# Attention's sums kept with heads on partitions, the division moved into the feed-forward on GpSimd

## The reference

```python
attend = (dist <= WINDOW) | glb[:, None] | glb[None, :]      # WINDOW = 128, glb: token 0
weights = softmax(where(attend, q @ k.T * SCALE, -inf))
x = x + (weights @ v) @ Wo.T                                 # q, k, v from layernorm(x)
h = bitlinear(xn, w_fc) + gate * (xn @ v.T @ fast_b.T @ u.T) # xn = layernorm(x)
x = x + bitlinear(relu(h) ** 2, w_proj)                      # bitlinear: ternary weights, scaled
```

## Time and profile before

| | |
|---|---|
| time, median of 3 runs (lowest to highest) | 1069.56 us (1068.85 to 1069.68) |
| the profiled execution | 1071.5 us |
| its span, first to last instruction | 1068.9 us |
| projection / attention / feed-forward, by TensorE's work | to about 190 / 190 to 702 / 702 to 1069 us |
| busy over the span: TensorE, VectorE, ScalarE, GpSimd | 1031.5, 921.4, 775.2, 699.6 us |
| mean granted TensorE clock | 0.995 of full speed |

### The profile page before, as it was taken

One profiled execution on the slowest core, in us unless ns is written; L12 is line 12 of the kernel. 1 busy time (PEld: TensorE's weight loads), 2 busy tenths in 40 slices (PEclk: granted clock), 3 DMA queues, 4 the chain that ended last, 5 costly groups with the idle time before them and its releaser, 6 DMA issues.

```text
span 1068.9 us, 40083 instructions
## 1 busy us (share of the span) xinstructions
PE 1031.5 (97%) x16071; PEld 789.2 (74%) x16071; DVE 921.4 (86%) x3202; ACT 775.2 (73%) x1328; POOL 699.6 (65%) x945
## 2 busy tenths in 40 slices
PE   9999999799999999999999999999999999999997
PEld 8888887466665666557665666588888888888886
DVE  7889987799999999999999999487888888888885
ACT  7989987687888888887888878854566554556554
POOL 3575556688888888898888888843344443344443
PEclk9999999899999999999999999999999999999999
DMA  6999989878667766776677653512122221123001
GB/s 210 263 314 276 286 231 267 155 136 154 129 139 156 157 126 137 158 145 130 139 138 160 131 120 70 143 38 80 59 89 90 60 60 60 60 79 95 26 21 40
DMA packets 187019, 142.33 MB, mean 133 GB/s; under 512 B 61625, under 2 KB 186577, under 8 KB 186833
## 3 DMA queue, kind: packets, MB, share of 16 engines
q1 hardware_dynamic: 186832, 139.77, 55.3%
HBM read 87.98 MB, written 50.95 MB: 130 GB/s over the span
## 4 chain that ended last, share of the span: by engine, by line
PE 60%; DVE 11%; issue 4%; SPq 3%; ACT 2%; DMA 1%; POOL 0%; DVEq 0%; ACTq 0%
PE e_psum L1616 13%; PE e_psum L1638 12%; PE e_psum L1347 9%; PE e_psum L1906 6%; PE e_psum L1908 6%; DVE a_masked L1362 4%; PE e_psum L1888 3%; PE e_psum L1887 3%; DVE n_stats L144 2%; DVE f_x L2028 2%; SPq L1321 2%; PE e_psum L231 1%; PE e_psum L233 1%; PE e_psum L232 1%; PE e_psum L1892 1%
## 5 line engine op out<-in xcount | busy, mean ns | idle before, releaser
L1692 ACT ACTIVATE a_weights<-e_psum 128x1024 f32<-128x1024 f32 (+1 forms) x512 | 391.4, 809 | 85.2 <-PE e_psum L1616 84.7
L1362 DVE CUSTOM_DVE_ANT_0 a_masked<-e_psum,band 128x290 f32<-128x290 f32 (+1 forms) x992 | 387.7, 445 | 37.9 <-PE e_psum L1347 32.1
L1526 POOL TENSOR_SCALAR_AFFINE_SELECT a_weights<-a_weights 128x1024 f32<-128x1024 f32 x256 | 273.9, 1094 | 48.6 <-ACT a_weights L1692 47.2
L1950 POOL TENSOR_TENSOR f_square<-f_relu 128x512 f32<-128x512 f32 x128 | 147.6, 1154 | 212.8 <-ACT f_relu L1939 189.6
L1347 PE MATMUL e_psum<-e_k,e_q 96*32 96x290 bf16 (+2 forms) x4096 | 236.5, 287 | 15.6 <-DVE max L1362 6.5
L1616 PE MATMUL e_psum<-e_q,e_k 128*32 128x384 bf16 (+2 forms) x5632 | 241.6, 280 | 5.8 <-ACT a_weights L1692 3.6
L1638 PE MATMUL e_psum<-a_weights,a_v 128*17 128x384 f32 (+2 forms) x2816 | 221.7, 389 | 2.0 <-issue 1.4
L1616 PEld LDWEIGHTS e_psum<-e_q,e_k 128*32 128x32 bf16 x5632 | 132.0, 96 | 97.0 <-ACT a_weights L1692 40.9
L1347 PEld LDWEIGHTS e_psum<-e_k,e_q 96*32 96x32 bf16 x4096 | 116.8, 97 | 84.1 <-DVE max L1362 46.7
L1906 PE MATMUL e_psum<-w_w_t,f_square_hi 128*128 128x256 f32 x512 | 129.4, 287 | 4.6 <-DVE f_square_lo L2004 4.6
L1939 ACT ACTIVATE f_relu<-e_psum,w_mag 128x512 f32<-128x512 f32 x128 | 87.4, 683 | 54.5 <-PE e_psum L1892 54.5
(11 more groups left out here) (215 smaller groups left out, 1925.3 us busy)
## 6 DMA issues: line engine op xcount, KB each, us to landing
k_parts<-p_k_parts SPq DMA_DIRECT2D x48, 258.0 KB, 4.7
q_parts<-p_q_parts SPq DMA_DIRECT2D x48, 256.0 KB, 5.5
e_q<-q_parts SPq DMA_DIRECT2D x64, 192.0 KB, 4.0
e_k<-k_parts SPq DMA_DIRECT2D x60, 193.5 KB, 3.7
v_ones<-p_va SPq DMA_DIRECT2D x16, 544.0 KB, 5.9
p_x<-in_x SPq DMA_DIRECT2D x16, 512.0 KB, 7.0
e_q<-q_parts SPq DMA_DIRECT2D x64, 128.0 KB, 3.9
f_o<-attention SPq DMA_DIRECT2D x16, 512.0 KB, 4.7
```

What stands on the lines that cost most here:

```text
L1362: dve.tensor_tensor_reduce(out=masked[:, place + lo:place + hi], in0=bank[:, lo:hi], in1=self.band[:, lo:hi], scale=1.0, scalar=NEG, op0=A ...
L1526: pool.affine_select(out=blocks, in_=blocks, compare_op=ALU.is_ge, fill=0.0, base=0, pattern=[[0, NQ // 2 * HEAD_COLS // P // CUT_STEP], [ ...
L1692: act.activation(pe_w[:, us.upar, lo:hi], score[c % 2][:], ACT.Exp).then_inc(s_exp, 1)
L1950: pool.tensor_tensor(sh.r2[:, j % 4, :], sh.r[:, j % 4, :], sh.r[:, j % 4, :], ALU.mult).then_inc(self.s_sq, 1)
```

## The change

The sum bank is no longer turned. It is copied as it lies to SBUF, by ScalarE for units with an even number (act_sums_copied) and by VectorE for those with an odd one, and stored to DRAM with heads and columns first, tokens last: 128 rows of 2 KB, one DMA a unit, denominators included. The weights of key 0 are turned for every pair of units on VectorE and stored too. GpSimd's L1538, L1540, L1554 and L1572 and VectorE's L1414 go.

The denominators are completed and inverted for many groups at once: those of the first three sequences around unit 51 (pool_den, dve_factor, pool_p0_factor, on 128 x 768 numbers), those of the last in the feed-forward (128 x 256). They go to DRAM and come back for each group as a factor of every row, repeated for the 16 columns of a head (load_factors, four DMAs of 256 KB), with load_o bringing the sums. GpSimd then combines (pool_combine): for each of the two halves of the columns, sums x factor, key 0's factor x its v, and their sum; for groups 0 to 2 in the last nine units of attention, for group i + 1 in feed-forward step i, one operation behind each of squares 1 to 6. This gives attention's result with columns on partitions, so pe_turn_o goes; ScalarE and VectorE make its high and low part from SBUF (act_o_high, dve_o_low), a step earlier than before. Half of attention's projection moves to where the turns stood. The diff, cut to the core:

```diff
+ROW0_STORED, FACTORS, COMBINED = 9, 50, UNITS - 9
+LAST_PARTS = 4
+
 L_MAX, L_SHIFT, L_SCORE, L_SUM, L_OUT = 2, 3, 5, 6, 7
+LEAD = 3
+COMBINE = 3 * KT
...
+    def pool_den(self, pool, last):
+        den, key0 = self.all_parts(last)
+        pool.wait_ge(self.s_parts, DMA * 2 * (B if last else B - 1))
+        pool.tensor_tensor(den, den, key0, ALU.add).then_inc(self.s_factor, 1)
+
+    def dve_factor(self, dve, last):
+        den = self.all_parts(last)[0]
+        dve.wait_ge(self.s_factor, 4 if last else 1)
+        dve.reciprocal(den, den).then_inc(self.s_factor, 1)
+
+    def pool_p0_factor(self, pool, last):
+        rden, key0 = self.all_parts(last)
+        pool.wait_ge(self.s_factor, 5 if last else 2)
+        pool.tensor_tensor(key0, key0, rden, ALU.mult).then_inc(self.s_factor, 1)
+
...
-    def dve_sums_turned(self, dve, u):
+    def dve_sums_copied(self, dve, u):
 
         dve.wait_ge(self.s_sum, u.n + 1)
-        wait(dve, self.s_den, u.n - 1)
-        wait(dve, self.s_num, u.n - 1)
-        dve.transpose(self.turned[:, u.upar].rearrange("p b e -> p (b e)"), self.sum_bank).then_inc(self.s_turned, 1)
-
...
+    def act_sums_copied(self, act, u):
+
+        act.wait_ge(self.s_sum, u.n + 1)
+        wait(act, self.s_out[u.upar], u.uhalf * DMA)
+        act.activation(self.sums[:, u.upar], self.sum_bank, ACT.Copy).then_inc(self.s_copied, 1)
+
...
+                if u := at(L_OUT):
+                    first = 1 if u.gi == 0 else 0
+                    sp.wait_ge(s_copied, u.n + 1)
+                    sp.dma_start(o_dram[u.g].rearrange("(a q) e t -> a q e t", q=UPG)[:, u.hq, :, first:GT],
+                                 sums[:, u.upar, first:GT]).then_inc(s_out[u.upar], DMA)
+                if (u := at(L_SCORE)) and u.n == FACTORS:
+                    sh.load_parts(sp, o_dram, p0_dram, range(B - 1))
+                if (u := at(L_SCORE)) and u.n == FACTORS + 3:
+                    sh.store_factors(sp, factor_dram, range(B - 1))
+                    feed.load_v0(sp, va_dram)
+                    feed.load_o(sp, Group(0))
+                    feed.load_o(sp, Group(1))
+                if (u := at(L_SCORE)) and u.n in (FACTORS + 4, FACTORS + 8):
+                    feed.load_factors(sp, Group((u.n - FACTORS) // 4 - 1))
...
-                if uo:
-                    pool.wait_ge(s_turned, uo.n + 1)
-                    pool.tensor_tensor(den[:, uo.upar], turned[:, uo.upar, :, HD], p0[:, uo.p0], ALU.add
-                                       ).then_inc(s_den, 1)
-                    pool.tensor_tensor(num[:, uo.upar], turned[:, uo.upar, :, 0:HD], t0[:, uo.n % 3], ALU.add
-                                       ).then_inc(s_num, 1)
+                if um and um.n >= 2:
+                    wait(pool, s_p0, um.n - 1)
+                    sh.pool_key0(pool, um, masked)
+                if us and us.gi == 0:
+                    pool.wait_ge(s_p0, us.n + 1)
+                    pool.tensor_tensor(p0[:, us.p0], p0[:, us.p0], gate0[:], ALU.mult).then_inc(s_gate, 1)
...
-                if uo:
-                    pool.wait_ge(s_num, uo.n + 1)
-                    pool.wait_ge(s_rden, uo.n + 1)
-                    if uo.hq == 0:
-                        wait(pool, s_out[uo.gpar], stored(uo))
-                    o = ob[:, uo.gpar, :, uo.hq * HD:(uo.hq + 1) * HD]
-                    pool.tensor_tensor(o, num[:, uo.upar], rden[:, uo.upar].unsqueeze(2).broadcast_to([P, SUBS, HD]),
-                                       ALU.mult).then_inc(s_o, 1)
-                if us and us.n < UNITS - 1:
-                    cut(us, 1, 0)
-                    cut(us, 1, 1)
+                    for half in range(2):
+                        cut(us, half, 0)
+                        cut(us, half, 1)
+                if us and us.n == FACTORS + 1:
+                    sh.pool_den(pool, False)
+                if us and us.n == FACTORS + 2:
+                    sh.pool_p0_factor(pool, False)
+                if us and us.n >= COMBINED:
+                    g, third = divmod(us.n - COMBINED, 3)
+                    for n in (2 * third, 2 * third + 1):
+                        feed.pool_combine(pool, Group(g), n)
...
+                if uo and not uo.last and uo.n < UNITS - 2:
+                    sh.act_sums_copied(act, uo)
...
+                if up and up.last:
+                    sh.dve_p0_turned(dve, up)
+                if uo and uo.last and uo.n < UNITS - 2:
+                    sh.dve_sums_copied(dve, uo)
+                if us and us.n == FACTORS + 2:
+                    sh.dve_factor(dve, False)
...
+    def load_factors(self, sp, q):
+
+        wait(sp, self.s_comb, q.g * COMBINE)
+        sp.wait_ge(self.sh.s_fout, DMA * 2 * (B if q.batch == B - 1 else B - 1))
+        for k in range(KT):
+            for which in range(2):
+                sp.dma_start(self.sh.factor[:, which, k],
+                             self.factor_dram[which, q.g, k * H // KT:(k + 1) * H // KT].unsqueeze(1)
+                             .broadcast_to([H // KT, HD, GT])).then_inc(self.s_fin_in, DMA)
...
+    def pool_combine(self, pool, q, n):
+
+        k, kind = divmod(n, 3)
+        o, rden, key0 = self.sh.o_t[:, q.par, k], self.sh.factor[:, 0, k], self.sh.factor[:, 1, k]
+        if kind == 0:
+            pool.wait_ge(self.s_oin[q.par], (q.half + 1) * KT * DMA)
+            pool.wait_ge(self.s_fin_in, (q.g + 1) * 2 * KT * DMA)
+            pool.tensor_tensor(o, o, rden, ALU.mult).then_inc(self.s_comb, 1)
+        elif kind == 1:
+            if q.g == 0:
+                pool.wait_ge(self.sh.s_v0, KT * B * DMA)
+            pool.tensor_tensor(key0, key0, self.sh.v0_t[:, k, q.batch:q.batch + 1].broadcast_to([P, GT]), ALU.mult
+                               ).then_inc(self.s_comb, 1)
+        else:
+            pool.wait_ge(self.s_comb, q.g * COMBINE + n)
+            pool.tensor_tensor(o, o, key0, ALU.add).then_inc(self.s_comb, 1)
+
...
     @block.gpsimd
     def _(pool):
-        for g in range(G):
+        def body(at):
+            qn, qf = at(-1), at(LF)
             for j in range(MH):
-                feed.pool_squares(pool, Group(g), j)
+                if qf:
+                    feed.pool_squares(pool, qf, j)
+                if qn and 1 <= j <= COMBINE:
+                    feed.pool_combine(pool, qn, j - 1)
+            if (q := at(0)) and q.g == LAST_PARTS + 1:
+                sh.pool_den(pool, True)
+            if (q := at(0)) and q.g == LAST_PARTS + 2:
+                sh.pool_p0_factor(pool, True)
+
+        steps(body)
 
     @block.tensor
     def _(pe):
...
             if qa:
-                feed.pe_turn_o(pe, qa, qf)
+                feed.pe_attention(pe, qa, (0,))
...
                 if j == 2 and qa:
-                    feed.dve_o_low(dve, qa)
+                    feed.dve_x1_half(dve, qa, 0)
+                if j == 6 and qn:
+                    feed.dve_o_low(dve, qn, (0,))
...
             if qx:
                 feed.dve_norm_low(dve, qx)
+            if qn:
+                feed.dve_o_low(dve, qn, (1,))
             if qa:
-                feed.dve_x1(dve, qa)
+                feed.dve_x1_half(dve, qa, 1)
```

332 lines of the change are left out of this document (161 added, 171 removed).

## The result

The changed kernel takes 1209.09 us (median of 4 runs, 1205.72 to 1215.53), against 1069.2 for the kernel before; the ratio is 1.132 (95% interval 1.126 to 1.137). The forecast was 1136 us, at most 1160. The profiled execution has a span of 1204.0 us, 135.1 more than before.

The account below looks back on a forecast made before the run. TensorE was taken to bound both stages, with GpSimd and VectorE taking turns in feed-forward steps after the change. Terms 59 - 2 - 2 + 2 + 5 + 1.5 + 3 = +66.5 on 1069.56 gave about 1136 us, range 1090 to 1160.

Parts of the forecast that it names:

- part 1: Thirteen feed-forward steps with combining: GpSimd and VectorE exclude each other and take turns, 27.6 us a step against 23.07; +59 us.
- rival (c): Feed-forward: a group's factors, asked for some 20 us into the step before, come late; 1156 us, chance 0.05.
- the signs named: Feed-forward steps of 27 to 28 us, low squares averaging 1.5 or more, TensorE near 80% busy; attention units at 7.6.
- part 2: TensorE's turns of attention's result go: -2 us in attention's tail, -2 in feed-forward steps not bound by combining.
- the reciprocal of 256 columns: Inverting the last batch's denominators at the start of a feed-forward step: 1.9 us long, +1 to +2 us.
- (a): Feed-forward: combining fits GpSimd's idle time and TensorE decides, 21.8 us a step; about 1061 us or 1050, chance 0.11.
- (b): Feed-forward: the engines' turns overlap and a step takes 25 us; 1102 us, chance 0.14.
- (d): Whole kernel: the terms cancel and the time stays the same; chance 0.02.
- part 4: Once-only work and transfers: +5 for a big reciprocal, +1.5 for the last, +3 for DMA issues, 0 for stores and loads.
- part 3: Attention's ordinary units: ScalarE's copies of sums start its first exp 0.15 us late; +2 us, bounds +5 and -10.
- The 18 issues: Attention, three units after unit 52: SP issues 18 DMAs in a row, 8 us in all; +3 us, 0 to 8.
- The reciprocal of 768 columns: Attention, unit 52: VectorE inverts three batches' denominators ahead of tiles TensorE waits for, 5.4 us; +5 us, bound below 0.9.

Follow-up runs that it names:

- the run with spare sums: The kernel before, with one unused GpSimd sum of 128x512 behind each of squares 1 to 6 in 13 feed-forward steps; 1131.07 us.
- the spread store: The changed kernel with each unit's 128 rows of sums stored to neighbouring DRAM rows, where before each head's 32 rows lay apart; 1176.27 us.

## Why the prediction was wrong

**What held.** What bounds the kernel in the feed-forward, and part 1's mechanism, the turns between the two engines. Its size, +59 for thirteen steps, came out by luck: measured, step by step against 23.07, are eleven times 3.73, 4.9 and 13.1, +59, in which two errors cancel. The ordinary step was forecast at 27.6 and is 26.80, though the combining's different-tile operations cost 1.26 and not 1.04, so the turns overlap more than the sum had it. And the first step takes 36.19, 9.4 more than the others, with TensorE waiting 6.98 us behind a late load of x, which no term and no rival had, and GpSimd 3.25 for factors, which is all that came of rival (c) in the feed-forward. Of the signs named, low squares have a mean of 1.07 us and not 1.5, and TensorE is busy 85% (363 of 425), not 80. The rest of part 2 and the reciprocal of 256 columns (+1.2; forecast +1 to +2) came out. Rivals (a), (b) and (d) are out: steps took neither 21.8 nor 25 us, and in the run with spare sums GpSimd's extra operations alone made 4.6 us a step.

**What failed** is one sentence of part 4: "The stores of sums double in bytes but go in rows of 2 KB; loads of 1 MB of factors a step lie in a stage whose DMA share is 0.20: 0." Neither got a bound, and this is why the range missed.
- The stores. They come with only two buffers and late in SP's queue, in the stage whose share is 0.68, not 0.20. Their price is the 19.7 us that the spread store takes off units 0 to 49, and by the traces some 10 more behind them (6.8 in the last units, 3.6 in the first feed-forward step, where the wait for x shrinks to 1.58). I judged them by bytes and row length; what counted was that their slowest dimension is 4, so that a store lands after 7.5 us and not 3.9. What is left of ordinary units is 3.9 us in 49, within part 3's bound of 5 and within what the same units vary.
- The factors of groups 0 to 2 are loaded in attention, 1 MB each, not in the feed-forward. The sum didn't have them at all. They cost 24 us in the last fourteen units.
- The 18 issues were put at +3, 0 to 8. They delay one pair's rows of shifts by 12 us. Eight of them gave 4 us (7 by the traces) with the factors' bytes out of the way and nothing with them there.
- The reciprocal of 768 columns was put at 5.4 us and took 4.95; the wait of 3.56 for GpSimd's sum in front of it was missed. Together 7.3 by the run without them (7.7 by its trace), for +5.

These runs account for about 20 of 24 us in ordinary units, and for 7 + 24 + 4 of the 58 in the last ones, where the spread store takes 6.8 too, if separate runs may be added. The other sixteen or so are not taken apart: the ten further issues, the wait of 10.74 us for group 2's sums, asked for in unit 61, and the slower clock after each stall.

## What to carry to other kernels

Read a new transfer's shape, not only its bytes: who carries it, what stands behind it in the same queue, and how many buffers wait for it; one edit of an address took 33 us off. Before work is moved to an idle engine, look at what stands beside the idle time: six GpSimd operations cost 5.2 us a step between the squares and 1.4 in the gap behind them. And read the one long step among equal ones by itself: here it hid an error of the forecast. Give a range to each term that is set to 0, above all in the stage where transfers are dense.

## What the hardware showed that I had not expected

- 256 KB stores with a slowest dimension of 4 landed 7.5 us after their issue (median) with five semaphore updates each, in a stretch with a DMA share of 0.62; the same bytes to 128 neighbouring rows landed after 3.9 us with sixteen, and 19 of 20 waits for them went. Their issue on SP took 0.57 us in the first form and 0.46 in the second (medians).
- 8 KB rows issued behind 1 MB of loads landed after 10 us, and after 3.3 when the loads were small.
- A GpSimd fill of 128x512 (0.53 us) holds up VectorE's tensor_scalar (0.69 us in place of 0.40 for one beside a fill alone) and not its subtraction of two SBUF tiles (0.68 us beside a fill, as with GpSimd idle).
- A GpSimd operation of 128x512 costs 1.04 us with one tile as both inputs or with a broadcast column as the second, and 1.26 with two full tiles.
